# The inverse of the 32x32 blocks spread over the four ticks by measured durations and begun behind the norms; its blocks loaded at the end of the fourth tick

## The reference, cut to what matters

```python
mixed = hidden_states @ w_qkv                  # then a causal convolution over 4 tokens and silu
q, k, v = split(mixed)                         # 16 heads of q and k, 32 heads of v, 128 wide
q = l2norm(q) * DK ** -0.5 ; k = l2norm(k)
def step(S, (q, k, v, g, b)):                  # 128 steps, one per token
    S = S * exp(g)
    delta = (v - k @ S) * b
    S = S + outer(k, delta)
    return S, q @ S
```

## Time and profile before

| | |
|---|---|
| median of the runs | 2197.31 us |
| the profiled execution | 2197.97 us |
| its span, first to last instruction | 2196.2 us |
| busy: TensorE, VectorE, ScalarE, GpSimd | 92%, 78%, 68%, 41% |
| mean granted TensorE clock | 0.969 |
| main loop in steady state | n = 8 to 63, about 160 to 1450 us of the span |

### The profile page before, as it was taken

How to read it: one execution, slowest core, us unless ns; L and a number is a source line. 1 busy time by engine, 2 the same in 40 slices (tenths; PEclk the granted TensorE clock), 3 DMA queues, 4 the chain that set the end, 5 groups by cost and what they waited for, 6 DMA issues and landing times.

```text
span 2196.2 us, 49295 instructions
## 1 busy us (share of the span) xinstructions
PE 2018.6 (92%) x18636; PEld 1681.6 (77%) x18636; DVE 1723.7 (78%) x2944; ACT 1497.9 (68%) x3523; POOL 893.3 (41%) x714
## 2 busy tenths in 40 slices
PE   4648999999999999999999999998878899999998
PEld 3437888888888888888888888887765567666676
DVE  6789798898988889898898988975236777767665
ACT  4536877778777787777878778765667666665632
POOL 1623454454454544544544545432343213322232
PEclk8869999999999999999999999998989999999999
DMA  3422323323233323323233232211342022222232
GB/s 79 96 70 50 81 57 69 83 55 67 63 74 71 68 65 67 74 65 75 64 61 79 63 70 71 42 49 48 87 148 87 1 97 73 82 96 97 83 129 87
DMA packets 274633, 161.56 MB, mean 74 GB/s; under 512 B 209352, under 2 KB 246752, under 8 KB 269280
## 3 DMA queue, kind: packets, MB, share of 16 engines
q1 hardware_dynamic: 274400, 158.41, 27.6%
HBM read 122.43 MB, written 35.91 MB: 72 GB/s over the span
## 4 chain that ended last, share of the span: by engine, by line
issue 35%; POOL 27%; PE 22%; DVE 9%; ACT 4%; DMA 2%; SPq 1%; POOLq 0%; DVEq 0%; ACTq 0%
POOL Q L557 5%; POOL SM L579 5%; POOL EB L495 5%; PE ps L1735 4%; POOL SZ L581 4%; PE ps L1351 3%; POOL EB L499 3%; PE ps L1352 2%; PE ps L1353 2%; POOL WL L473 2%; POOL SM L587 2%; ACT SC L860 2%; PE ps L1647 1%; PE ps L1656 1%; PE ps L1484 1%
## 5 line engine op out<-in xcount | busy, mean ns | idle before, releaser
L913 DVE SCALAR_TENSOR_TENSOR A<-ps,CW,A 128x508 f32<-128x508 f32 (+2 forms) x768 | 517.1, 735 | 62.7 <-ACT A L676 59.9
L574 POOL TENSOR_SCALAR SM<-SM 128x8 f32<-128x8 f32 x64 | 12.7, 198 | 746.8 <-ACT DL L695 746.8
L1351 PE MATMUL ps<-XH,WH 128*128 128x512 f32 x512 | 223.2, 436 | 31.9 <-DVE A L913 31.0
L1484 PE MATMUL ps<-WO,DL 128*128 128x256 f32 x1008 | 232.7, 384 | 19.0 <-ACT DL L682 11.6
L1484 PEld LDWEIGHTS ps<-WO,DL 128*128 128x128 f32 x1008 | 193.3, 193 | 47.9 <-ACT DL L682 13.4
L1353 PE MATMUL ps<-XH,WL 128*128 128x512 f32 x512 | 208.1, 407 | 0.0
L1352 PE MATMUL ps<-XL,WH 128*128 128x512 f32 x512 | 207.5, 405 | 0.0
L695 ACT ACTIVATE DL<-SZ 128x128 f32<-128x128 f32 x512 | 152.9, 300 | 59.4 <-issue 32.6
L1131 DVE TENSOR_TENSOR SZ<-SZ,ps 128x512 f32<-128x512 f32 x128 | 86.6, 687 | 128.4 <-PE ps L1520 126.9
L860 ACT ACTIVATE SC<-ps,A 128x128 f32<-128x128 f32 x512 | 142.2, 387 | 51.3 <-DVE A L1256 50.7
L1116 DVE TENSOR_TENSOR BP<-ps,EB 128x512 f32<-128x512 f32 x256 | 158.4, 682 | 2.6 <-ACT EB L667 2.6
(11 more groups left out here) (223 smaller groups left out, 5530.7 us busy)
## 6 DMA issues: line engine op xcount, KB each, us to landing
EB<-decay_rows SPq DMA_DIRECT2D x128, 256.0 KB, 4.6
WE<-expert_halves SPq DMA_DIRECT2D x32, 1024.0 KB, 5.1
x_blocks<-BP SPq DMA_DIRECT2D x256, 32.0 KB, 1.7
X<-x_blocks SPq DMA_DIRECT2D x16, 512.0 KB, 5.8
tt_blocks<-TI SPq DMA_DIRECT2D x16, 512.0 KB, 2.6
tn_blocks<-TM SPq DMA_DIRECT2D x16, 512.0 KB, 2.6
TTF<-tt_blocks SPq DMA_DIRECT2D x256, 32.0 KB, 1.9
expert_halves<-BP SPq DMA_DIRECT2D x8, 1024.0 KB, 5.5
```

Source lines behind the costliest of these rows:

```text
L913: dve.scalar_tensor_tensor(acc, ps(i, 0, [[128, 4], [1, 128 - s]]), at(CW, tile * 4 + 3 - s, [[1, 1]]), acc, ALU.mult, ALU.add).then_inc(s ...
L1351: pe.matmul(out, sa, ma, start=(kt == 0), stop=False)
L1484: t = pe.matmul(ps(7 - i, b * 256, [[1, 256]]), at(on_buf(k), (4 * i + 2 * b + v) * 128, [[1, 128]]), at(WO, v * 256, [[1, 256]]), start=( ...
```

## The change

Six edits, none of which changes what is computed:

1. The prices of the inverse's instructions become 150 + 1.05 N ns for a product and 180 + 1.72 N for a reduce.
2. From n = 8 on, the inverse is appended directly behind `norm_sums` in ticks with n % 4 == 0, ahead of the pump that stands before `v_tap` 1. That pump's room is 4100 (was 2500 and 1560), the one after `v_tap` 3 is 700 (was 500), the one behind `y_add` 2900 (was 2000). With the new prices the 40 yields fall: tick 0: 18, 1, 2; tick 1: 4, 1, 2; tick 2: 4, 2, 3; tick 3: 3, -, -. In the ticks from n = 64 on the room doubles (`rate`), as before.
3. TensorE transposes the norm rows ahead of `v_proj(vn, 0)` instead of between its two halves.
4. ScalarE writes the transposed copy behind the silu of v instead of between the two halves of `on_T`.
5. `store_t` is split in two, `store_t` and `store_tn`. On SP, in ticks with n % 4 == 3, the two stores, `load_ta`, and `load_tt` come behind `store_x` and `load_rows`. `load_tt` does so in every tick after the first of them.
6. `load_x` is issued in the tick with n % 4 == 3, between `load_ta` and `load_tt`, instead of at the head of the next tick.

```diff
--- before.py
+++ after.py
@@ -324,6 +324,8 @@
                     if j >= 2:
                         sp.wait_ge(sem["ld_tt"], 256 * (j - 1))
                     sp.dma_start(tt_scr[j % 2].rearrange("c i s t -> (c i) (s t)"), at(TI, 0, full)).then_inc(sem["st_t"], 16)
+
+                def store_tn(j):
                     sp.wait_ge(sem["tn"], j + 1)
                     if j >= 2:
                         sp.wait_ge(sem["ld_ta"], 192 * (j - 1))
@@ -396,23 +398,31 @@
                     vn, wn = m + 1, m + 2
                     if 0 < k < NSTEP and k % 4 == 0:
                         load_wo(k // 4)
-                    if n % 4 == 0 and 4 <= n <= NSTEP:
-                        load_x(n // 4 - 1)
                     if 0 <= m < NSTEP and m % 4 == 1 and m // 4 + 1 < HK:
                         load_z(m // 4 + 1)
                     if n % 4 == 1 and n // 4 + 1 < HK:
                         load_kq(n // 4 + 1)
                     if 0 <= vn < NSTEP and vn % 4 == 1 and vn // 4 + 1 < HK:
                         load_v(vn // 4 + 1)
-                    if 0 <= wn < NSTEP and wn % 4 == 0:
-                        store_t(wn // 4)
-                    if 0 <= wn < NSTEP:
+                    if 0 <= wn < NSTEP and wn % 4:
                         load_ta(wn)
-                        load_tt(wn)
+                    if wn == 0:
+                        store_t(0)
+                        store_tn(0)
+                        load_ta(0)
+                        load_tt(0)
                     if n < NSTEP:
                         store_x(n)
                     if n + 3 < NSTEP:
                         load_rows(n + 3)
+                    if 0 < wn < NSTEP and wn % 4 == 0:
+                        store_t(wn // 4)
+                        store_tn(wn // 4)
+                        load_ta(wn)
+                    if n < NSTEP and n % 4 == 3:
+                        load_x(n // 4)
+                    if 0 < wn < NSTEP:
+                        load_tt(wn)
                     if n == NSTEP + 2:
                         load_raw(0)
                         load_raw(1)
@@ -808,9 +818,6 @@
                         decay_exp(n + 1)
                     if s4 and k < NSTEP - 1:
                         on_T(k, 0)
-                    if 0 <= wn < NSTEP and wn % 4 == 0:
-                        act.wait_ge(sem["inv"], INV_OPS * (wn // 4 + 1))
-                        act.activation(at(TM, 0, [[1, 32], [32, 32]]), at(TI, 0, [[32, 32], [1, 32]]), ACT.Copy).then_inc(sem["tn"], 1)
                     if s4 and k < NSTEP - 1:
                         on_T(k, 1)
                     if EARLY <= n and n % 2 == 0 and n + 1 < NSTEP:
@@ -820,6 +827,9 @@
                     if sv:
                         act.wait_ge(sem["v_conv"], 6 * vn + 6)
                         act.activation(at(A2, 0, full), at(A2, 0, full), ACT.Silu).then_inc(sem["v_silu"], 1)
+                    if 0 <= wn < NSTEP and wn % 4 == 0:
+                        act.wait_ge(sem["inv"], INV_OPS * (wn // 4 + 1))
+                        act.activation(at(TM, 0, [[1, 32], [32, 32]]), at(TI, 0, [[32, 32], [1, 32]]), ACT.Copy).then_inc(sem["tn"], 1)
                     if s3:
                         if s4:
                             act.wait_ge(sem["out_mm"], 2 * k + 2 if m < NSTEP - 1 else 2 * k)
@@ -921,6 +931,12 @@
 
                 inv = sem["inv"]
 
+                def mult_ns(n):
+                    return 150 + 1.05 * n
+
+                def sum_ns(n):
+                    return 180 + 1.72 * n
+
                 def inverse(j):
                     dve.wait_ge(sem["ld_xb"], 16 * (j + 1))
                     dve.wait_ge(sem["rk"], j + 1)
@@ -950,12 +966,12 @@
                             dve.wait_ge(inv, done)
                             dve.tensor_tensor(at(TM, o, dims[0]), at(X, xo, dims[1]), at(TI, to, dims[2]), ALU.mult).then_inc(inv, 1)
                             done += 1
-                            yield 100 + nb * s * s * s // min(nb, s)
+                            yield mult_ns(nb * s * s * s // min(nb, s))
                         dve.wait_ge(inv, done)
                         dve.tensor_reduce(at(UT, 0, [[1, nb * s * s]]), at(TM, 0, mid), AX.X, ALU.add,
                                           negate=False).then_inc(inv, 1)
                         done += 1
-                        yield 100 + nb * s * s * s
+                        yield sum_ns(nb * s * s * s)
                         for it in range(min(nb, s)):
                             if nb <= s:
                                 o, xo, to = it * s ** 3, it * blk + s * 33, it * s * s
@@ -966,24 +982,24 @@
                             dve.wait_ge(inv, done)
                             dve.tensor_tensor(at(TM, o, dims[0]), at(TI, xo, dims[1]), at(UT, to, dims[2]), ALU.mult).then_inc(inv, 1)
                             done += 1
-                            yield 100 + nb * s * s * s // min(nb, s)
+                            yield mult_ns(nb * s * s * s // min(nb, s))
                         dve.wait_ge(inv, done)
                         dve.tensor_reduce(at(TI, s, [[blk, nb], [32, s], [1, s]]), at(TM, 0, mid),
                                           AX.X, ALU.add, negate=True).then_inc(inv, 1)
                         done += 1
-                        yield 100 + nb * s * s * s
+                        yield sum_ns(nb * s * s * s)
                     for q4 in range(4):
                         k0, kn = 4 * q4, 16 - 4 * q4
                         dve.wait_ge(inv, done)
                         dve.tensor_tensor(at(TM, 0, [[16 * kn, 4], [16, kn], [1, 16]]), at(X, k0 * 32 + 16, [[0, 4], [32, kn], [1, 16]]),
                                           at(TI, k0 * 32 + k0, [[32, 4], [1, kn], [0, 16]]), ALU.mult).then_inc(inv, 1)
                         done += 1
-                        yield 100 + 64 * kn
+                        yield mult_ns(64 * kn)
                         dve.wait_ge(inv, done)
                         dve.tensor_reduce(at(UT, k0, [[1, 4], [16, 16]]), at(TM, 0, [[16 * kn, 4], [1, 16], [16, kn]]), AX.X,
                                           ALU.add).then_inc(inv, 1)
                         done += 1
-                        yield 100 + 64 * kn
+                        yield sum_ns(64 * kn)
                     for q4 in range(4):
                         i0, kn = 4 * q4, 4 * q4 + 4
                         dve.wait_ge(inv, done)
@@ -1172,12 +1188,13 @@
                         norm_rows(n - 1)
                     if n % 4 == 0 and 4 <= n <= NSTEP:
                         norm_sums(n // 4 - 1)
-                    pump(2500)
-                    pump(1560)
+                        if n >= EARLY:
+                            under_way.append(inverse(n // 4 - 1))
+                    pump(4100 if EARLY <= n < NSTEP else 0 if n == NSTEP else 5800 // rate)
                     if sv:
                         v_tap(vn, 1)
-                    if n % 4 == 0 and 4 <= n <= NSTEP:
-                        under_way.append(inverse(n // 4 - 1))
+                    if n == 4:
+                        under_way.append(inverse(0))
                     if sv:
                         v_tap(vn, 2)
                     if n < EARLY:
@@ -1191,14 +1208,12 @@
                         v_tap(vn, 3)
                     if n == 0:
                         decay_base(1)
-                    pump(500)
-                    if n % 4 == 3:
-                        pump(50000)
+                    pump(50000 if n % 4 == 3 else 700)
                     if s4 and k < NSTEP - 2:
                         y_add(k, 0)
                     if s4 and k < NSTEP - 2:
                         y_add(k, 1)
-                    pump(2000)
+                    pump(2900)
                     if s3:
                         gate(m, 0)
                     if s3:
@@ -1558,9 +1573,10 @@
                                 t = pe.matmul(ps(6 + i, pr * 32, [[1, 32]], 64 * i, 32), at(U1, pr * 32, [[1, 32]], r0, 32),
                                               tt(vn, pr * 128 + r0, [[1, 32]], r0, 32), start=True, stop=True)
                         t.then_inc(sem["tt64"], 1)
-                        v_proj(vn, 0)
                     if n % 4 == 0 and 4 <= n <= NSTEP:
                         norms_tr(n // 4 - 1)
+                    if sv:
+                        v_proj(vn, 0)
                     if sv:
                         v_proj(vn, 1)
                     if m == NSTEP - 1:
```

## The result

The changed kernel takes 2345.99 us (median of four runs, 2341.21 to 2347.92), the kernel before 2198.51 (four runs, 2196.64 to 2201.70): a ratio of 1.0666 [1.0644, 1.0688]. The forecast was 2342. The profiled execution has a span of 2342.9 us against 2196.2, and a mean granted clock of 0.944 against 0.969.

What follows compares the result with a forecast made beforehand. PE bounds the loop; from 2198.0 us, the delayed block with low clock +122, late TA +49, spread inverse -21 and ends -6 sum to 2342 us. Its own range is 2315 to 2375; the 8-in-10 range 2225 to 2378.

Steps and rivals of the forecast that it cites:

- part 2: Tick 0, ahead of v_tap 1: the inverse's block collides with POOL; PE's kq projection stands 6.9 us per period.
- Part 5: SP's queue in tick 3: row loads hold the stores, TA lands late, PE stands 3.8 us at u1, 13 times.
- Part 6: Ramp and tail of the kernel: 6 us gained in all (bounds 0 and -10).
- 1, norms_tr early: Tick 0: norms_tr ahead of v_proj ends the norms 1.5 us earlier, at no cost.
- Part 3: Behind PE's stop at the kq projection: the granted clock falls to 0.50, adding 1.8 us per period.
- 4, rest of the inverse: Ticks 1 to 3: the lighter spread of the inverse takes away 1.5 us of PE waits per period.
- bare block: Tick 0: the inverse's block runs unhindered by POOL, costing 0.4 us per period, TA still late; 2225 us, chance 0.06.
- stores not held: SP's queue in tick 3: rows don't delay the stores, so late TA costs 1.1 us; 2307 us, chance 0.16.
- half lock: Tick 0 block: two products fit between POOL's instructions, PE stands 3.9 us, clock costs 1.7; 2298 us, chance 0.13.
- Faster: Ticks 2 and 3: PE's two waits close, with a bare block and TA early; 2181 us, chance 0.08.

Runs made afterwards that it cites:

- experiment 8: The kernel before with only norms_tr moved ahead of v_proj: 2199.32 us, ratio 1.0011.
- experiment 2: The changed kernel with SP's order, load_x and ScalarE's transposed copy as before, the early inverse and new prices kept: 2293.44 us, ratio 1.0445.
- experiment 3: The changed kernel with four POOL instructions in ticks with n%4 = 0 cut to a few elements (results not the reference's): 2271.26 us, one run.
- experiment 1: The changed kernel with the inverse placed and priced as before, SP's new order and ScalarE's late copy kept: 2283.94 us, ratio 1.0389.
- experiment 4: The changed kernel with tick 3's load_rows issued behind the stores, load_ta and load_x: 2299.26 us, one run.
- experiment 5: The changed kernel with ScalarE's transposed copy back between the two halves of on_T: 2332.34 us, ratio 1.0617.
- experiment 6: The changed kernel with row loads behind the stores and four POOL instructions cut short (results not the reference's): 2244.27 us, ratio 1.0214.
- experiment 7: The changed kernel with row loads behind the stores, four POOL instructions cut short, and load_tt ahead of load_x and the rows: 2211.70 us, ratio 1.0068.

## Why the prediction was right

The mechanism held in every step. The sizes held too, three of them in part by luck (parts 2, 5 and 6, below). Step by step, in us per period but for the last row:

| step | predicted | measured | shown by |
|---|---|---|---|
| 1, norms_tr early | 0 | 0 (2199.3 against 2196.6 in all) | experiment 8 |
| 2, block beside POOL | 6.9, v_tap 1 at T+18.5 | 6.76, v_tap 1 at T+18.4 with u1's stop taken off | experiments 2 and 3 |
| 3, low clock behind it | 1.8 | 1.98 | stretches of tick 0 |
| 4, rest of the inverse | -1.5 | -1.62 (0.64 in tick 2, 0.98 in tick 3) | ticks 1 to 3 |
| 5, TA late | 3.8 | 3.91 | experiments 1 and 4 |
| 6, ends, in all | -6 | about -4 | below |

The changed kernel is behind the one before, read at u1, by 7.7 us at n = 12, 139.5 at n = 60, 147.9 at n = 61, and 146.9 at the end: 11.0 per period in the middle, and 14 blocks with 13 stops for TA as counted. 14 x (6.76 + 1.98 - 1.62) + 13 x 3.91 = 150.5, which leaves -3.6 for the ends.

The waits that were to show it: L1366 for v_tap 3 has 99.2, but 31.0 of it were there before, so the new part is 68 where "some 90" stood; the rest is the 2.06 per period that the low clock hid. For TA it is 65.4, 13.3 of it from before, so 52 where "some 50" stood.

Six things went otherwise than worked out, without moving the sum much:

- Part 3 put the low clock behind the second stop alone. It falls behind u1's stop as well, where it costs nothing only because v_tap 3 is later still. With the block away (experiment 1) it costs 2.3 per period, so the rivals with a bare block and TA late were some 13 x 2.3 = 30 us too low.
- Inside the block, L935 and the third small product were to wait for POOL's scaling of z and L473. The low clock delayed the norms by more than the shift, the scaling was done, and the block took 9.6 us and not 12. That it still ended within 0.1 us of the forecast is luck: less u1's stop, POOL's series ended at T+17.2 in the mean and not at 15.9, and 1.2 us of the block stood behind it and not 2.6. Experiment 2, with u1 on time, shows the layout as it had been worked out: POOL done at T+15.8, v_tap 1 at T+18.4, a stop of 6.58.
- Part 5 had the copy's new place matter only up to the rows. Experiment 5 shows that TA is in 0.7 later for it.
- Two more sizes of part 5 were off and cancel. The stores went out at T+18.8 and not 17.8, and the one of TM landed at T+25.6 and not 24.6; from there TA's loads were in after 2.7 us and not 3.8. So the 3.91 against 3.8 is luck in part.
- load_tt was left in the range with up to 0.9. In the changed kernel TTF is not late; with u1 on time it is, by 2.0 to 3.3 (experiments 4 and 6). It is a third cost that the first one covers.
- Part 6 had some 4 us gained in the tail and 2 in the ramp. The traces show the ramp alone: from one u1 to the next, tick 9 took 24.05 us before, with the stop and the low clock of the earlier trace rows, and 20.40 after, with a stop of 1.68 and the clock up. In the tail, ticks 65 and 66 are 6.6 us shorter, but ticks 63, 68 and 69 are 5.0 longer and the rest some 1.0.

The rival "stores not held" (2307) fell with experiment 4, "half lock" (2298) with the 6.76 and the products of experiment 2, "bare block" with the same. "Faster" asked for TA early and a bare block; experiment 7 has nearly both, and is still 0.7% slower than before.

On the lock the Trainium skill (SBUF — State Buffer, "Who interferes with whom") says that a VectorE instruction with two SBUF inputs and a GpSimd one that reads SBUF block each other for the whole instruction, and a reduce never does. The runs agree: four such products take 3.55 us with POOL's work beside them and 1.04 without, the reduce behind them 0.61 in both.

How the rows hold the stores can be read from the traces of the changed kernel and of experiments 1 and 5: in all three store_t lands 1.3 us behind the second row load and store_tn 1.2 behind store_t (means, n = 15 to 59), whenever they were issued. So what counts is when the row loads land. Why they land later where ScalarE's copy is late is open, and so is whether X or the rows held TTF. Neither was tried.

## What to carry to other kernels

Prices taken from bare durations place small two-input VectorE products where a busy POOL makes them three to nine times dearer; look at POOL's timeline in the stretch before moving them ahead of a deadline. A store moved behind loads on one queue hands their time to whoever reads it back, so the deadline to check is the reader's, a tick later. A forecast that lands on the number is not yet right in its parts: only experiment 2 shows the block as it had been laid out. Where a stop is taken away, look for the one that it covered: in tick 0 there were three (TA, TTF, v_tap 3), and the low clock behind each.

## What the runs showed of the hardware

- VectorE's small products got through one or two per POOL instruction, whatever their own size: 3.55 us for four of 64 elements beside POOL's 1.34, 1.90 and part of 1.92, where four took 1.00 with POOL at rest; 3.09 for two of 32 (experiment 2), which take 0.42 bare.
- The granted clock was 0.51 to 0.57 after PE's stops of 3.96, 4.46 and 2.38 us, for 3.3 to 6.9 us. After stops of 1.76 us it stayed at 1.00 (experiment 7). Between these it went both ways: low after 1.94 (experiment 7, n = 56) and up after 2.59 (experiment 1, n = 56).
- A store of 512 KB landed in 2.6 us. Behind two row loads of 256 KB it landed in 4.6 to 6.2 (medians of the changed kernel and experiments 1, 3 and 5), 1.3 and 2.5 us behind the second of them.
